# First pair of tables selected one table at a time, the third tile's layer 2 split around layer 1, and the bias of layer 2 added by VectorE for three tiles

## The reference

```python
e = jnp.stack([tbl_0[ids[:, 0]], ..., tbl_25[ids[:, 25]]], axis=1)
combined = jnp.concatenate([r_dense_features[:, None, :], e], axis=1)      # 512 x 27 x 128
interactions = jnp.einsum('bfd,bgd->bfg', combined, combined)
z = interactions[:, iu, ju]                                                # pairs f < g
h = jnp.concatenate([z, r_dense_features], axis=1)                         # 512 x 479
h = jnp.maximum(h @ W_top1 + b_top1, 0.0)                                  # 512
h = jnp.maximum(h @ W_top2 + b_top2, 0.0)                                  # 256
y = h @ W_top3                                                             # 512 x 1
```

## Time and profile before

| | |
|---|---|
| median of 3 runs | 109.31 us (109.14 to 109.95) |
| the profiled execution, device time | 109.58 us |
| its span in the trace | 107.8 us |
| mean granted TensorE clock over the span | 1.0 of full speed |
| busy share: PE, PEld, DVE, ACT, POOL | 94%, 76%, 62%, 54%, 59% |
| gathers issued by POOL | 56 |

### The profile page before, as it was taken

The page is one execution under the profiler, slowest core; times in us unless marked ns, Lnnn a source line. Parts: engine busy times, 40 slices in busy tenths (PEclk is TensorE's granted clock), DMA queues, the critical chain, the costliest instruction groups (busy, mean ns, idle before and its releaser), DMA issues.

```text
span 107.8 us, 3434 instructions
## 1 busy us (share of the span) xinstructions
PE 101.7 (94%) x1497; PEld 81.5 (76%) x1497; DVE 66.9 (62%) x113; ACT 57.7 (54%) x84; POOL 63.8 (59%) x63
## 2 busy tenths in 40 slices
PE   4989999999999999999999999999999999969981
PEld 4666886888888888889998976787777696659860
DVE  1599959999999699999012957665222722162232
ACT  1795933299983795999444179460015600341210
POOL 2877787777877787877777777877775000000000
PEclk9999999999999999999999999999999999999999
DMA  2999789999999999684111112211222000000000
GB/s 53 295 279 230 222 207 241 217 227 212 229 236 225 240 244 291 187 257 136 47 56 49 30 49 55 55 49 49 55 55 65 14 0 6 6 0 0 6 0 1
DMA packets 5885, 13.13 MB, mean 122 GB/s; under 512 B 1783, under 2 KB 2697, under 8 KB 5870
## 3 DMA queue, kind: packets, MB, share of 16 engines
q1 hardware_dynamic: 3018, 8.37, 30.7%
q0 software_dynamic: 1792, 3.67, 13.7%
q10 hardware_dynamic: 1060, 0.87, 3.8%
HBM read 12.89 MB, written 0.01 MB: 120 GB/s over the span
## 4 chain that ended last, share of the span: by engine, by line
PE 92%; DVE 3%; issue 1%; ACT 1%; POOL 0%; DVEq 0%; POOLq 0%
PE banks L390 27%; PE banks L452 11%; PE banks L411 8%; PE banks L431 6%; PE banks L373 5%; PE banks L483 4%; PE banks L336 3%; PE banks L489 3%; PE banks L363 3%; PE banks L515 3%; PE banks L484 3%; PE banks L460 2%; PE banks L348 2%; PE banks L516 2%; PE banks L522 2%
## 5 line engine op out<-in xcount | busy, mean ns | idle before, releaser
L327 POOL DMA_INDIRECT rows<-in_tbl,ids_sb x56 | 63.0, 1126 | 18.1 <-issue 16.8
L390 PE MATMUL banks<-onehots,tab_hi 125*128 125x512 f32 x64 | 25.3, 395 | 0.0
L390 PE MATMUL banks<-onehots,tab_lo 125*128 125x512 f32 x64 | 25.0, 390 | 0.0
L668 ACT ACTIVATE tab_hi<-stage 125x1024 fp32r<-125x1024 f32 (+1 forms) x12 | 12.3, 1024 | 9.8 <-PE banks L390 3.9
L877 DVE COPY_PREDICATED picked<-second_of,banks 128x112 f32<-128x112 int32 x16 | 4.3, 281 | 20.6 <-ACT picked L729 19.1
L847 DVE TENSOR_TENSOR tab_lo<-stage,tab_hi 125x1024 fp32r<-125x1024 f32 x12 | 14.3, 1214 | 1.8 <-ACT tab_hi L668 1.8
L452 PEld LDWEIGHTS banks<-feats 128*27 128x27 f32 x1024 | 10.9, 104 | 5.1 <-DVE picked L877 2.2
L860 DVE TENSOR_SCALAR onehots<-ids_bc,row_of 125x1024 fp32r<-125x1024 f32 x21 | 14.4, 750 | 0.7 <-PE banks L373 0.5
L860 DVE TENSOR_SCALAR onehots<-ids_bc_h,row_of 125x1024 fp32r<-125x1024 int16 x21 | 14.4, 753 | 0.0
L729 ACT ACTIVATE picked<-banks 128x112 f32<-128x112 f32 x16 | 4.1, 261 | 18.9 <-PE banks L452 18.8
L390 PEld LDWEIGHTS banks<-onehots,tab_hi 125*128 125x128 f32 x64 | 12.0, 188 | 2.8 <-issue 0.4
(11 more groups left out here) (85 smaller groups left out, 151.1 us busy)
## 6 DMA issues: line engine op xcount, KB each, us to landing
stage<-in_tbl SPq DMA_DIRECT2D x11, 448.0 KB
stage<-in_w SPq DMA_DIRECT2D x3, 512.0 KB
rows<-in_tbl,ids_sb POOLq DMA_INDIRECT x56, 6.6
ids_bc_h<-ids_short_rows ACTq DMA_DIRECT2D x6, 128.0 KB, 8.6
stage<-in_tbl SPq DMA_DIRECT2D x11, 52.0 KB
stage<-in_tbl SPq DMA_DIRECT2D x2, 224.0 KB
dense_sb<-in_dense SPq DMA_DIRECT2D x1, 256.0 KB, 11.4
stage<-in_w SPq DMA_DIRECT2D x1, 256.0 KB
```

Source lines behind the costliest of these rows:

```text
L327: nc.gpsimd.indirect_dma_start(out=rows[:, t % RB, m, :], out_offset=None, in_=tables[m], in_offset=bass.IndirectOffsetOnAxis(ap=ids_sb[:, ...
L390: last = nc.tensor.matmul(bank(n, k), tab_part(i, part)[:, c, :], onehots[0:RP, c, k, :], start=(c == 0 and part == 0), stop=(c == CHUNKS ...
L668: nc.scalar.activation(tab_part(i, 0)[:, first:, :], src[:, first:, :], ACT.Copy).then_inc(hi_ready, 1)
```

## The change

Three edits, and what each does:

- **First pair.** The one-hots of step 0 are made table by table, in operations of 512 columns instead of 1024, on VectorE (chunks 0 to 6) and ScalarE (chunk 7). TensorE does the rounded part of table 0, then that of table 1, each chunk as its one-hot comes; then `spread_ids(1)`; then the two low parts. The filler transposes are gone. ScalarE's order in the start changes with it: `make_hi(2)` now stands ahead of `copy_ids(1)`.
- **Bias of layer 2.** For tiles 0 to 2 there is no bias matmul. The bias is loaded once, broadcast to all partitions (`b2_bc`, a third small DMA on SP behind a wait for the last one-hots), and VectorE adds it from PSUM into SBUF ahead of the relu and sum of `finish`. Tile 3 keeps the bias matmul.
- **Order at the end.** `layer2_hi` of tile 2 stands right behind `move_picked` of tile 3. Its `layer2_lo` follows the second half of layer 1 of tile 3, and the second half's transposes of tile 3 come directly behind it, ahead of the bias matmul and layer 2 of tile 3.

```diff
             def select_first():
-                pe.wait_ge(half_hi_ready, 1)
-                for c in range(CHUNKS):
-                    if c == CHUNKS // 2:
-                        pe.wait_ge(hi_ready, 1)
-                        spread_ids(1)
...
-                    nc.tensor.matmul(bank(0, 0), tab_part(0, 0)[:, c, :], onehots[0:RP, c, 0, :], start=(c == 0),
-                                     stop=False)
-                    if c < CHUNKS - 1:
-                        warm_up(FILL)
-                for k, part in ((1, 0), (0, 1), (1, 1)):
...
+                for k, part in ((0, 0), (1, 0), (0, 1), (1, 1)):
+                    if part == 1:
+                        pe.wait_ge(lo_ready, k + 1)
+                    elif k == 1:
+                        pe.wait_ge(hi_ready, 2)
+                    else:
+                        pe.wait_ge(half_hi_ready, 1)
+                    if (k, part) == (0, 1):
+                        spread_ids(1)
                     for c in range(CHUNKS):
+                        if (k, part, c) == (0, 0, CHUNKS // 2):
+                            pe.wait_ge(hi_ready, 1)
+                        if part == 0 and c < CHUNKS - 1:
+                            pe.wait_ge(onehot_by_dve if k == 1 else first_by_dve, c + 1)
+                        elif part == 0:
+                            pe.wait_ge(onehot_by_act if k == 1 else first_by_act, 1)
...
+            sp.wait_ge(onehot_by_dve, by_dve(NSTEP - 1, CHUNKS - 2))
+            sp.wait_ge(distance_ready, NSTEP)
+            sp.dma_start(b2_bc, b2[0, :].partition_broadcast(P)).then_inc(small_loaded, 16)
...
             def layer2_start(t, acc):
                 if t == 0:
-                    pe.wait_ge(bias_ready, 1)
-                    pe.wait_ge(ones_ready, 1)
+                    pe.wait_ge(ids_copied, BY_DMA)
                     pe.wait_ge(lo_ready, S + WV + 1)
                 elif t < T - 1:
-                    pe.wait_ge(y_ready, t)
+                    pe.wait_ge(sums_biased, t)
                 else:
+                    pe.wait_ge(bias_ready, 1)
+                    pe.wait_ge(ones_ready, 1)
                     pe.wait_ge(picked_by_dve, U * t + 3)
-                nc.tensor.matmul(acc, ones[:], b2_rows[:], start=True, stop=False)
+                    nc.tensor.matmul(acc, ones[:], b2_rows[:], start=True, stop=False)
...
             last_layer1_dense()
+            layer2_start(T - 2, l2_ps[:, 0:H2])
             move_picked(T - 1)
+            layer2_hi(T - 2, l2_ps[:, 0:H2])
             last_layer1_hi(0)
             last_layer1_lo(0)
             last_layer1_hi(1)
             last_transpose_hidden(0)
             last_layer1_lo(1)
-            layer2(T - 2)
+            layer2_lo(T - 2, l2_ps[:, 0:H2])
+            last_transpose_hidden(1)
             layer2_start(T - 1, l2_last[:, 0:H2])
             layer2_hi(T - 1, l2_last[:, 0:H2], range(0, CH))
-            last_transpose_hidden(1)
             layer2_lo(T - 1, l2_last[:, 0:H2], range(0, CH))
...
             copy_ids(0)
             make_first_half_hi()
             make_hi(0)
-            make_distance(0)
-            make_last_onehot(0)
+            make_first_last_onehot(0)
             make_hi(1)
+            make_first_last_onehot(1)
+            make_hi(2)
             copy_ids(1)
-            make_hi(2)
             make_distance(1)
...
+            def make_first_onehots(k):
...
+                    nc.vector.tensor_scalar(onehots[0:RP, c, k, :], ids_bc[0][0:RP, k, :], row_of[:, c:c + 1], None,
+                                            ALU.is_equal).then_inc(first_by_dve if k == 0 else onehot_by_dve, 1)
...
                 dve.wait_ge(layer2_done, t + 1)
-                acc = l2_ps if t < T - 1 else l2_last
-                nc.vector.scalar_tensor_tensor(h2w3, acc[:, 0:H2], 0.0, w3_bc[:], ALU.max, ALU.mult,
+                acc = l2_last[:, 0:H2]
+                if t < T - 1:
+                    nc.vector.tensor_tensor(biased, l2_ps[:, 0:H2], b2_bc, ALU.add).then_inc(sums_biased, 1)
+                    dve.wait_ge(sums_biased, t + 1)
+                    acc = biased
+                nc.vector.scalar_tensor_tensor(h2w3, acc, 0.0, w3_bc[:], ALU.max, ALU.mult,
                                                accum_out=y[:, t:t + 1]).then_inc(y_ready, 1)
```

More of the change, by code:

```diff
@@ L514, in layer2_hi @@
                 for c in pieces:
-                    nc.tensor.matmul(acc, h1T_hi[t % 2][:, c, :], w2_hi[:, c, :], start=False, stop=False)
+                    nc.tensor.matmul(acc, h1T_hi[t % 2][:, c, :], w2_hi[:, c, :], start=(t < T - 1 and c == 0),
+                                     stop=False)
                     nc.tensor.matmul(acc, h1T_hi[t % 2][:, c, :], w2_lo[:, c, :], start=False, stop=False)
@@ L690, in make_last_onehot @@
                 act.wait_ge(distance_ready, n + 1)
-                if n >= 1:
-                    act.wait_ge(onehot_used, used(n - 1, CHUNKS - 1))
+                act.wait_ge(onehot_used, used(n - 1, CHUNKS - 1))
                 nc.scalar.activation(onehot(n, CHUNKS - 1), distance[0:RP, 0:len(steps[n]), :], ACT.Relu, scale=-1.0,
```

62 lines of the change are left out of this document (36 added, 26 removed).

## The result

| | before | whole change |
|---|---|---|
| median of 5 runs on the same chip | 109.81 us (109.14 to 111.27) | 108.09 us (107.78 to 109.72) |
| ratio, 95% interval | | 0.9876 [0.9836, 0.9916] |
| profiled execution: time, span | 109.58, 107.8 us | 107.98, 106.2 us |

So the change gives 1.4 us, between 0.9 and 1.8, where 2.5 had been forecast; 108.09 is 0.09 above the range. The ratio leaves out one disturbed run of the change (109.72).

The account below looks back on a forecast made before the run. TensorE was taken to bound nearly the whole span, its in-order queue limited at the last group by POOL's gathers. Gains 0.35 + 0.45 + 1.7 = 2.5 from 109.58 gave 107.1, or 106.8 by the median; forecast 107.0, range 106.0 to 108.0.

Parts of the forecast that it names:

- 1. The first pair: Ahead of the last gather: narrower one-hots let step 1 start at 17.3 instead of 18.21, gain 0.9 us.
- The price of a one-hot: First pair on VectorE: a 512-column one-hot taken as 0.40 us, between bounds of 0.34 and 0.68.
- What reaches the end of 1 and 2 together: Last group's transposes: TensorE 1.35 us early, but rows land at 84.97, so start near 85.05 and gain 0.35.
- rival C: Gather stream: VectorE's 0.8 us longer first pair delays the last landing and all behind by 0.8; 107.9, chance 0.08.
- 0.94 us each: POOL's 56 gathers: issued back to back at this length, with 0.30 us of issue between.
- the 0.45 us between landing and transposes: Last gathered group: lands 84.97, transposed from 85.42; savings ahead of that are worth at most this much.
- 2. The bias matmuls: Layer 2: each removed bias matmul saves 0.45 us; tile 1's, behind the last gather, counts in full.
- 3. The end: Reordered end: last two low matmuls start at 102.7 instead of 104.40, gain 1.7 us.
- Rival B: The end: ScalarE and VectorE get the second half one behind the other, half of 1.7 lost; 107.9, chance 0.12.
- A: Last gather: lands earlier and doesn't hold TensorE, so 1.0 us more comes through; 106.1, chance 0.10.
- D: First pair: half a one-hot costs a whole one, step 1 starts 1.9 us later; 108.9, chance 0.07.
- E: First pair: without fillers TensorE stays at 1.2 GHz, step 1 3.0 us late; 110.0 or more, chance 0.03.

Follow-up runs that it names:

- pair_only: The kernel before with the first pair's edit alone; median 110.49 us, ratio 1.0046 to the kernel before.
- no_last_third: The whole change without the last six gathers (tile 3's last two groups) and their wait, so old rows are transposed; ratio 0.9856 to the kernel before.
- order_only: The kernel before with the new order at the end alone, all bias matmuls kept; median 107.69 us, ratio 0.9827 to the kernel before.
- bias_order: The whole change without the first pair's edit (bias on VectorE and new end order only); median 107.86 us, ratio 0.9805 to the kernel before.
- wide_third: The whole change with one-hots of 1024 columns on VectorE in the first pair; ratio 0.9971 to the kernel before.
- wide_onehots: Same kernel as wide_third, run on chips where the kernel before takes 138 to 140 us; ratio 0.9837, and 0.9879 on another.
- no_fill: The kernel before without its fourteen filler transposes, on a chip where before takes 138 to 140 us; ratio 0.9958.

## Why the prediction was wrong

**1. The first pair: gain 0.9, measured 0.34.** The price of a one-hot was right (0.40), so was the start of TensorE (5.61 for 5.75). The step that failed is "VectorE ends the fourteenth at 10.7; the last two chunks of table 1 follow by 11.4 ... spread_ids takes 0.65: 12.05 ... The low part of table 0 ... doesn't hold". It does: in the diff the wait for the low part stands ahead of spread_ids(1), and the first subtraction ends at about 11.7 (10.53 + 3.49 / 3), so the spread starts at 11.80 and ends at 12.52, 0.47 later than forecast. In TensorE's timeline of pair_only the wait is named:

```profile
11.77 0.71 PE L350 MATMUL banks<-pairs_hi,ident_r 12*128 12x512 f32 x2 [0.40 <-DVE tab_lo L857]
```

The chain behind it was right: from the spread's end to step 1 there are 5.35 (12.52 to 17.87), and 5.25 were forecast (12.05 to 17.3).

**What reaches the end of 1 and 2 together.** This is the step that made the number wrong: "TensorE would stand at the last group 1.35 early, at 84.07. The rows land at 84.97; it starts at about 85.05. Gain 0.35." It starts at 86.29, a loss of 0.87. Both halves failed. The last gather is issued 1.9 later (83.69 for 81.77) and lands 2.6 after that, so the rows come at 86.3, 1.3 later than 84.97, since the first pair's operations on VectorE stretch gathers. The direction of rival C was right, with 1.9 us at the issue and 1.3 at the landing for my 0.8, and "the trace shows no gather that a VectorE row delays" was a misreading, as the trace of before has such gathers (below). So was "0.94 us each": that is the last one, and the mean of the 56 is 1.13 on the page. But the late rows are not what cost most of the time, as no_last_third shows. TensorE was not early either: the pair products of tiles 0 to 2 took back what the first pair and the bias had given. I had summed stages as if what is saved ahead of an unchanged stretch of one engine arrived at its end in full, and put the stops inside that stretch at nothing.

The 0.87 can be added up: 0.34 and 0.45 saved as above and 0.05 more on the way to g(0,0), against 0.32 of waiting for the rows and 1.35 of stops inside blocks from g(0,0) to these transposes (2.48 us in the whole change, 1.12 before). That makes 0.83. Nor was the 0.45 us between landing and transposes firm: with the same instructions until 95 us, order_only issued its last gather at 80.78, 1.0 earlier than before.

**2. The bias matmuls: right in place and size.** 0.45 to 0.50 in the two stages that lose one (5.85 to 5.37 or 5.40; 6.50 to 6.00 in bias_order). VectorE's added operation stayed covered. In the time the sum of it doesn't show: bias_order's g(2,0) to g(2,3) is 6.76 where order_only has 6.33, again pair products: a stop of 1.09 at instruction 1984, where order_only has 0.81, and one more of 0.20.

**3. The end: right.** 1.7 forecast, 1.68 in the profile, and 1.9 (1.4 to 2.4) by the times of order_only alone, whose profile has 1.65 there. Rival B falls: the operand of the last part comes at 101.32 + 0.38 = 101.70, forecast 101.66, and no gap over 0.3 stands in front of its matmuls.

**Rivals.** A (106.1) and D (108.9) fall: the gathers came later and the one-hots cost 0.40. E falls here, with matmuls at full clock by 12.45, but wide_third shows it to be real: without fillers and with wide one-hots the level rises some 5 us later. C gives 107.9, nearest to 108.09, by a wait that makes up some 0.3 us of the loss: a right time for a mostly wrong reason, so luck.

**What stays open.** That the pair products slow down by stops inside their blocks is shown, that these stand at fixed counts and at fixed points of POOL's rounds too, and that they go with the first pair's edit: 15.37 to 16.00 in the six kernels that have it, 14.45 to 14.81 in the three without. order_only differs from before by 0.34 in that stage with the same instructions in it, and 0.31 of that are stops that go with gathers, so some of it varies from one execution or build to the next. What happens at a fixed count is an inference: TensorE's instructions come in blocks of 256, and small matmuls, which use them up fastest, reach the next block before it is there. The Trainium skill, "Advanced Engine Details and Errata", ISA Cache, gives a line of 256 instructions, and the trace agrees with that number (1984 and 2240, and the transfers of 16 KB). How a gather stops TensorE no run here shows. And no run on a chip at 109 to 110 us put the fillers' count back, so the us that this alone would return are not measured.

## What to carry to other kernels

A saving ahead of a long stretch of small matmuls isn't a saving until the end of that stretch has been seen to move. In such a stretch look at the start times one by one: stops of 0.1 to 1 us hide in it, and taking fourteen instructions out ahead of it moved them. Measure each part alone, as the part that looks like a gain of 0.9 was a loss of 0.5. What was moved into the last idle gap of the program, behind which nothing can take it back, came through in full. Of the kernels tried, the best have the end's new order and leave the first pair as it was (0.9827 with the order alone, 0.9805 with the bias edit too).

## What the runs showed of the hardware

**A gather issued during a VectorE operation with two SBUF inputs ends 0.8 us after that operation, in the rows below.** In the whole change the three subtractions end at 10.53 + 3.49 = 14.02 and the gather at 10.64 + 4.19 = 14.83. The kernel before has the same, in its POOL timeline:

```profile
11.06 1.97 POOL L327 DMA_INDIRECT rows<-in_tbl,ids_sb  x1 [0.30 <-issue]
...
37.12 1.80 POOL L327 DMA_INDIRECT rows<-in_tbl,ids_sb  x1 [0.30 <-issue]
```

and in VectorE's:

```profile
36.87 1.23 DVE L847 TENSOR_TENSOR tab_lo<-stage,tab_hi 125x1024 fp32r<-125x1024 f32 x1 [0.88 <-ACT tab_hi L668]
```

38.92 is 0.82 after 38.10, and 13.03 is 0.83 after 12.20, the end of the second subtraction of the earlier trace rows. One-hots stretch a gather too, from 0.94 to 1.02 with 1024 columns and to 1.28 with 512; back to back narrow ones held one gather of pair_only from 7.45 to 10.71, 0.1 behind the last of them, and such a gather of 3.26 stands there in eight of the eleven profiles with narrow ones. In the other three it takes 1.28 or 1.68. The profile of the whole change above is one of these three, and its repeat on another chip is one of the eight, so this comes and goes between executions. The Trainium skill, "SBUF — State Buffer", SBUF: two separate sides, says that a DMA issued by GpSimd can't have its descriptors written while VectorE holds the shared ports in a two-port mode, but counts an operation with two SBUF inputs as a conflict only against GpSimd instructions that read SBUF. The one-hots, 1024 columns in 0.68 where a subtraction of as many takes 1.22, would fit the first half. The subtractions are of the second kind. The gathers take their row numbers from `ids_sb`, which lies in SBUF, so the rows, which show them held, agree with that if this counts as reading; no run here tried a DMA of POOL that reads none.

**The clock.** Behind narrow one-hots and without fillers the trace gives 2.4 GHz from 7.2 to 10.5 us on (eleven profiles). The kernels with before's first pair and its fillers have it from 8.7 to 9.4 (four profiles; bias_order has no record), and wide one-hots without fillers only from 13.1 to 14.8 (four profiles: wide_onehots 13.1, its repeat 14.4, wide_third 14.7, no_fill 14.8).

**TensorE's stops.** They are told above: at instruction counts 256 apart, 1.24 to 1.60 us after a transfer on the instruction queue, and at three points of POOL's round of 1.25 us while gathers are issued.
